# Denominators a pair later in an attention kernel: both late key sums on VectorE, the shift spread on ScalarE, and another order at the seams

## The reference, cut to what matters

```python
x = x + 0.5 * ffn(layernorm(x))
x = x + attn(layernorm(x))
x = x + 0.5 * ffn(layernorm(x))

# attn: 16 heads of 64
q = q * cos + rotate_half(q) * sin + fenc
k = k * cos + rotate_half(k) * sin + fenc
dots = einsum('bhid,bhjd->bhij', q, k) * 64 ** -0.5
attn = softmax(dots, axis=-1)
out = einsum('bhij,bhjd->bhid', attn, v)
return out.reshape(b, n, 1024) @ w_out.T + b_out
```

## Time and profile before

| what | value |
|---|---|
| median of 3 runs (lowest, highest) | 1273.29 us (1272.16, 1274.07) |
| the profiled execution's own time | 1275.4 us |
| its span in the profile | 1273.6 us |
| PE busy | 1229.2 us, 97% |
| DVE busy | 955.6 us, 75% |
| POOL busy | 896.2 us, 70% |
| ACT busy | 627.9 us, 49% |
| chain that ended last | PE 86%, issue 4%, POOL 4%, DVE 3% |

### The profile page before, as it was taken

One profiled execution on the slowest core, in us unless ns is written; L12 is line 12 of the kernel. 1 busy time (PEld: TensorE's weight loads), 2 busy tenths in 40 slices (PEclk: granted clock), 3 DMA queues, 4 the chain that ended last, 5 costly groups with the idle time before them and its releaser, 6 DMA issues.

```text
span 1273.6 us, 20947 instructions
## 1 busy us (share of the span) xinstructions
PE 1229.2 (97%) x7346; PEld 780.9 (61%) x7346; DVE 955.6 (75%) x1443; ACT 627.9 (49%) x917; POOL 896.2 (70%) x652
## 2 busy tenths in 40 slices
PE   4999999899999999999999999999999987999998
PEld 3666666556666566666666666666666644666665
DVE  6656777778888888888888888888787865656632
ACT  3444522455555546455556555555555552443422
POOL 0443346788998898898898899889889932543353
PEclk9999999999999999999999999999999998999999
DMA  5353150132333333232323232323232310443150
GB/s 169 134 183 91 43 150 17 33 66 54 70 58 67 61 64 64 63 65 59 69 60 68 60 68 60 68 57 70 51 77 52 76 19 19 141 142 108 43 158 17
DMA packets 118677, 95.35 MB, mean 75 GB/s; under 512 B 75760, under 2 KB 85008, under 8 KB 118320
## 3 DMA queue, kind: packets, MB, share of 16 engines
q1 hardware_dynamic: 118064, 93.75, 30.2%
q10 hardware_dynamic: 512, 0.26, 0.1%
HBM read 57.53 MB, written 2.88 MB: 47 GB/s over the span
## 4 chain that ended last, share of the span: by engine, by line
PE 86%; issue 4%; POOL 4%; DVE 3%; DMA 1%; ACT 1%; SPq 0%; POOLq 0%; DVEq 0%; ACTq 0%
PE banks L1156 16%; PE banks L453 15%; PE banks L1135 13%; PE banks L466 10%; PE banks L1074 6%; PE banks L994 5%; PE banks L1172 5%; PE banks L1140 4%; PE banks L1181 4%; PE banks L1002 3%; POOL work L1428 2%; PE banks L1113 1%; POOL turn L1418 1%; PE banks L415 1%; PE banks L408 1%
## 5 line engine op out<-in xcount | busy, mean ns | idle before, releaser
L1006 DVE TENSOR_REDUCE neg_max<-banks 128x2 f32<-128x1024 f32 x256 | 305.1, 1226 | 11.0 <-PE banks L994 6.2
L1256 ACT ACTIVATE work<-banks 128x1024 f32<-128x1024 f32 x256 | 262.4, 1026 | 93.8 <-PE banks L1140 77.6
L1156 PE MATMUL banks<-work 128*64 128x512 f32 x1024 | 233.8, 598 | 2.0 <-ACT work L1256 1.1
L1428 POOL TENSOR_TENSOR work<-work 128x1024 f32<-128x1024 f32 x64 | 159.6, 2494 | 81.4 <-PE banks L1156 81.3
L1418 POOL TENSOR_TENSOR turn<-turn,side_turned 128x512 f32<-128x512 f32 x128 | 163.7, 1301 | 29.8 <-DMA side_turned<-side 29.6
L1412 POOL TENSOR_TENSOR turn<-turn,fenc 128x512 f32<-128x512 f32 x128 | 162.8, 1291 | 2.0 <-DVE side L1327 2.0
L1423 POOL TENSOR_TENSOR qk_l<-turn,qk_h 128x512 fp32r<-128x512 f32 x128 | 161.8, 1285 | 2.8 <-ACT qk_h L983 2.8
L1156 PEld LDWEIGHTS banks<-work 128*64 128x64 f32 x1024 | 68.0, 136 | 135.0 <-issue 109.9
L1348 DVE TENSOR_TENSOR work<-work 128x1024 f32<-128x1024 f32 x64 | 105.4, 1647 | 38.2 <-PE banks L1156 38.2
L807 POOL TENSOR_TENSOR o_raw<-o_raw,work 128x512 f32<-128x512 f32 x52 | 66.9, 1289 | 89.8 <-DVE o_raw L723 89.7
L807 POOL TENSOR_TENSOR work<-work 128x512 f32<-128x512 f32 x44 | 56.5, 1292 | 96.7 <-DVE work L723 51.7
(11 more groups left out here) (177 smaller groups left out, 2459.3 us busy)
## 6 DMA issues: line engine op xcount, KB each, us to landing
work<-share SPq DMA_DIRECT2D x32, 1024.0 KB, 9.4
side_turned<-side SPq DMA_DIRECT2D x256, 128.0 KB, 3.1
rec_all<-rec_d SPq DMA_DIRECT2D x128, 128.0 KB, 3.0
x_tok<-in_x SPq DMA_DIRECT2D x8, 256.0 KB, 6.5
out<-x_tok SPq DMA_DIRECT2D x8, 256.0 KB, 9.4
work<-in_w_gate_up SPq DMA_DIRECT2D x1, 1280.0 KB, 7.2
work<-in_w_qk SPq DMA_DIRECT2D x1, 1024.0 KB, 9.7
den_d<-den_rows ACTq DMA_DIRECT2D x64, 4.0 KB
```

What stands on the lines that cost most here:

```text
L1006: return nc.vector.tensor_reduce(neg_max[:, g % 2, qt::DH], of, AX.X, ALU.max, negate=True)
L1156: ins = nc.tensor.matmul(o_bank(g)[OWN[h], :], v_all[:, kt, n * DH:(n + 1) * DH], pt[:, g % 2, kt, h * T:(h + 1) * T], start=(kt == 0), st ...
L1256: nc.scalar.activation(pt[:, g % 2, kt, :], S[kt].rearrange("p h q -> p (h q)"), ACT.Exp, scale=QSCALE).then_inc(s["probs"], 1)
L1428: nc.gpsimd.tensor_tensor(pt[:, g % 2, 2, :], pt[:, g % 2, 2, :], pt[:, g % 2, 3, :], ALU.add).then_inc(s["second_sum"], 1)
```

## The change

It has these parts, of which the first four are in the attention stage.

- The denominators of pair `g` are formed a period later (in period `g+2`), from one tile instead of two, for all pairs but the last two (`lazy`). VectorE adds tile 3 to tile 2 (`late_sum`, after V has been applied to these two, which now come first in `ORDER`), GpSimd adds tile 1 to tile 0 into tile 3 (`early_sum`), and in the next period VectorE adds tile 3 to tile 2 again (`total`). TensorE multiplies tile 2 alone with ones.
- Everything behind the denominators moves a period later too: copying, DMAs, reciprocals, normalising, output projection, residual. `o_raw` has three places for that.
- `spread_maxima` moves from VectorE to ScalarE, as four activations of 128 columns.
- In period 61 the odd tokens of `ffn2`, and at the program's start those of `ffn1`, move from VectorE (`first_tokens`) to ScalarE (`odd_tokens`).
- The order at the seams: positions and shares of the routing one unit later, routing steps spread over other units, the early layer norm one unit sooner, and another order in attention's tail.

```diff
-LOGITS_AT, EXPS_AT, POSITIONS_AT, SHARES_AT = 8, 10, 14, 16
+LOGITS_AT, EXPS_AT, POSITIONS_AT, SHARES_AT = 8, 10, 15, 17
-FIRST_ROUTE_AT = {0: range(4, 12), 1: range(12, 19), 2: range(19, 22), 3: range(22, 24)}
+FIRST_ROUTE_AT = {0: range(4, 12), 1: range(12, 19), 2: range(19, 22), 4: range(22, 24)}
-        o_raw = sb("o_raw", [P, 2, T])
+        o_raw = sb("o_raw", [P, 3, T])
-            first_positions, first_shares = (1, 2) if last else (3, 4)
+            first_positions, first_shares = (2, 3) if last else (4, 5)
...
+                def odd_tokens():
+                    act.wait_ge(s["normed"], 1)
+                    for t in range(TT):
+                        n = TT + t
+                        ins = nc.scalar.activation(xn2[1][:, t, :], x_tok[:, 1, t, :], ACT.Identity,
+                                                   scale=rs_c[:, n:n + 1], bias=shift_c[:, n:n + 1])
+                    ins.then_inc(s["xn_first"], 1)
...
-            EARLY_NORM_AT = {-14: range(0, 4), -13: range(4, 7), -12: range(7, 10), -11: range(10, 13), -10: range(13, 16)}
+            EARLY_NORM_AT = {-15: range(0, 4), -14: range(4, 7), -13: range(7, 10), -12: range(10, 13), -11: range(13, 16)}
...
+            ORDER = (2, 3, 0, 1)
+
+            def lazy(g):
+                return g < N - 2
...
                 def denominators(g, p):
                     pe.wait_ge(s["v_ready"], min(p + 4, B * 2 * TT))
                     at_least(pe, s["den_copied"], g)
-                    pe.wait_ge(s["first_sum"], g + 1)
-                    pe.wait_ge(s["second_sum"], g + 1)
-                    for n, kt in enumerate((0, 2)):
+                    if lazy(g):
+                        pe.wait_ge(s["total"], g + 1)
+                    else:
+                        pe.wait_ge(s["late_sum"], g + 1)
+                        pe.wait_ge(s["early_sum"], g + 1)
+                    tiles = (2,) if lazy(g) else (2, 3)
+                    for kt in tiles:
...
-                    if exists(p - 3):
-                        project_out(p - 3, p)
-                    if exists(last):
-                        denominators(last, p)
+                    if exists(p - 4):
+                        project_out(p - 4, p)
...
+                    if exists(p - 2):
+                        denominators(p - 2, p)
...
+                def spread_maxima(g):
+                    act.wait_ge(s["shift_ps"], g + 1)
+                    at_least(act, s["scores"], (g - 1) * TT)
+                    for t in range(TT):
+                        ins = nc.scalar.activation(shift[:, g % 2, t * P:(t + 1) * P], MT, ACT.Copy, scale=own_rows[:, t:t + 1])
+                    ins.then_inc(s["shift_ready"], 1)
...
-                def first_sum(g):
-                    dve.wait_ge(s["first_applied"], g + 1)
-                    nc.vector.tensor_tensor(pt[:, g % 2, 0, :], pt[:, g % 2, 0, :], pt[:, g % 2, 1, :],
-                                            ALU.add).then_inc(s["first_sum"], 1)
+                def add_tiles(g):
+                    return nc.vector.tensor_tensor(pt[:, g % 2, 2, :], pt[:, g % 2, 2, :], pt[:, g % 2, 3, :], ALU.add)
+
+                def late_sum(g):
+                    dve.wait_ge(s["last_applied"], g + 1)
+                    add_tiles(g).then_inc(s["late_sum"], 1)
+
+                def total(g):
+                    dve.wait_ge(s["early_sum"], g + 1)
+                    dve.wait_ge(s["late_sum"], g + 1)
+                    add_tiles(g).then_inc(s["total"], 1)
...
-                    if exists(p - 2):
-                        reciprocals(p - 2)
+                    if exists(p - 3):
+                        reciprocals(p - 3)
+                    if exists(p - 2):
+                        total(p - 2)
                     end_norm(p)
...
                     if exists(p - 1):
-                        first_sum(p - 1)
-                    if exists(nxt):
-                        spread_maxima(nxt)
+                        late_sum(p - 1)
...
-                def second_sum(g):
+                def early_sum(g):
                     pool.wait_ge(s["o_ps"], g + 1)
-                    nc.gpsimd.tensor_tensor(pt[:, g % 2, 2, :], pt[:, g % 2, 2, :], pt[:, g % 2, 3, :],
-                                            ALU.add).then_inc(s["second_sum"], 1)
+                    pool.wait_ge(s["late_sum"], g + 1)
+                    nc.gpsimd.tensor_tensor(pt[:, g % 2, 3, :], pt[:, g % 2, 0, :], pt[:, g % 2, 1, :],
+                                            ALU.add).then_inc(s["early_sum"], 1)
```

136 lines of the change are left out of this document (73 added, 63 removed).

## The result

The changed kernel takes 1326.04 us (median of 4 runs, 1322.95 to 1327.34), the kernel before 1272.80 in the runs beside it: a ratio of 1.0412, 95% interval 1.0393 to 1.0431. The forecast was 1296 with a range of 1275 to 1318. Sign and mechanism came out as argued; the time lies outside the range.

What follows compares the result with a forecast made beforehand. TensorE bounds the kernel before, GpSimd second; after the change, GpSimd and VectorE's sums in turn. 1275.4 + 25.6 + 7 - 9.9 = 1298.1 us, less 2.1 for the median: 1296 us, range 1275 to 1318.

Steps and rivals of the forecast that it cites:

- (1): TensorE in attention: half the denominator matmuls go in 62 lazy pairs, saving 0.45 us a period, hidden behind GpSimd.
- (2): Attention: VectorE's second key sum also blocks GpSimd for 1.00 us, making the period 13.27 us, +25.6 us in all.
- No order of the instructions gets below this sum: Attention: GpSimd and VectorE are served in turn, so reordering cannot bring the period below 13.27 us.
- the front term: Seven batch-turning periods: spreading on ScalarE delays rope, residual and TensorE by 1.0 us each, +7 us, bounds 0 and 11.
- The upper bound of the term: Attention: each VectorE sum costs GpSimd its full 1.22 us, giving +51 us instead of +25.6.
- Before: 11.27 + 1.00 = 12.27: Kernel before, attention: GpSimd's work plus one blocking sum stays under the 12.83 us period, hidden in 1.39 us of waits.
- the second sum finds 0.39 us of them: Attention: GpSimd's gaps already hide the first VectorE sum, leaving 0.39 us for the second; argued against a faster result.
- case C: Rival, about as now: full seam gains, cheaper sums or VectorE's total landing in GpSimd's waits; 1262 to 1272 us, chance 0.06.
- (3): Attention: spreading on ScalarE takes 1.4 us and delays the seven batch-turning periods, +7 us.
- (5): Seams at the program's start and attention's ends: reordering removes TensorE waits, -9.9 us in sum.
- (4): Attention: third raw-output buffer, reciprocals and normalising a period later remove VectorE's waits for DMA; counted as nothing.
- case A: The forecast itself: GpSimd and VectorE's sums in turn set the period at 13.0 to 13.4 us; 1281 to 1304, chance 0.72.

Runs made afterwards that it cites:

- e3: The changed kernel with VectorE's `total` replaced by a one-operand reduction over as many columns, part of the denominators left out: 1271.66 us, ratio 0.9973.
- e6: The kernel before with one more VectorE addition of two SBUF operands, 1024 columns, per period, result unused: 1309.93 us, ratio 1.0272.
- e7: The kernel before with one more VectorE reduction of one SBUF operand, 1024 columns, per period, result unused: 1275.76 us, ratio 1.0010.
- e15: The changed kernel with GpSimd's Fourier additions cut to half the positions, the rest left out: 1282.99 us, ratio 1.0073.
- e5: The changed kernel with a buffer of its own for GpSimd's sum, which no longer waits for the late sum: 1323.32 us, ratio 1.0392.
- e14: The changed kernel with VectorE's late sum put ahead of the total: 1315.44 us, ratio 1.0326.
- e4: The changed kernel with the spreading of the maxima back on VectorE: 1317.78 us, ratio 1.0349.
- e11: The kernel before with part of the change's seams, the last `first_sum` between routing steps, positions and shares later in `ffn2`: 1269.24 us, ratio 0.9965.
- e12: The kernel before with one more VectorE addition of two SBUF operands, only 512 columns, per period, result unused: 1286.31 us, ratio 1.0109.

## Why the forecast had the sign and not the size

By its own terms, against the profiled executions. The forecast's sum for the changed kernel, 1298.1 us, stands against 1324.93: 26.8 us short.

- **(1) Half the denominators' matmuls.** Forecast 0.45 us a period, hidden. Found: it comes to light only when GpSimd is relieved (e3's median period 12.35).
- **(2) Two meetings set the period, 13.27 us, +25.6.** The mechanism is shown from both sides: e6 and e7 by adding it, e3 by taking it away, e15 by the load. Its price is right too, if both forms of it are counted: in the change GpSimd is blocked for 1.20 us a period and waits 0.83 for the late sum, 2.03 for the 2.00 taken. What failed is the step "No order of the instructions gets below this sum", read as if the kernel could also reach it: the sum 11.27 + 2.00 has no other wait of GpSimd, while the forecast's own sign allowed up to 25 us of them. Found were 19.4 us in the stretch, 0.33 a period: 12.6 for the turned side, 4.9 for TensorE, 1.9 for rope. The table below has this split for five kernels. With the 7 of the front term, which is one of these waits, 12.4 us were missing, and 1.8 more for the 2.03: 14.2 us of the shortfall. The upper bound of the term (1.22 us a sum, +51) would have covered the stretch, though for another reason.
- **A price misread in the kernel before.** "Before: 11.27 + 1.00 = 12.27" is not what its rows say: GpSimd was busy for 663.22 us, 11.43 a period. The first sum had hardly used the slack of 1.39, so "the second sum finds 0.39 us of them" is wrong as well. The error does not touch the 13.27, but it hid that the cost of a meeting depends on who is loaded.
- **The new wait.** The forecast did not name the wait of GpSimd's sum for the late sum in its sum (case C touches it). It is GpSimd's longest (48.3 us). By itself it is not the cause, as e5 shows; its order relative to the total is worth 0.16 us a period (e14).
- **(3) Spreading on ScalarE.** Its four instructions of 372 ns each overlap and take 1.13 us (1.4 taken). The +7 us for the seven periods that turn a batch was nearly right, and by the path that was forecast as far as rope: by e4, 5.6 us. On TensorE they do not stand out (13.79 us in the mean, the others 13.62), since the delay reaches it a period later through GpSimd and not through the residual.
- **(5) The seams, -9.9.** Found: -1.8 ahead of the stretch and +4.5 behind it, +2.7, so 12.6 us of the shortfall. Single executions scatter here: the ten kernels with lazy pairs have 268.36 to 270.65 us ahead of the stretch, 269.7 in the mean, the four with the old order 270.7, so the gain is nearer 1.0 than 1.8. One term was misread from the start: at the program's start the odd tokens do not move to ScalarE (only in period 61), against what the change's description says further up, and the +1.5 for it never was; TensorE's first projection waits 1.5 us for `x_lo` as before. The mask's wait falls from 2.1 to 1.3. At the far end "each wait may have another behind it" was the right doubt with too small a price: the four waits of 8.4 us went, and 9.7 and 3.6 came. Without the lazy pairs this end does give what was forecast (e11, -7.0 behind the stretch for the -6).
- **(4)** was costed at nothing, "waits of an engine off the bound", and the DMAs were said to "cover themselves". That holds in the steady stretch; it fails in the tail, where the order on SyncE and the place of pair 61's reciprocals on VectorE make the 9.7 us.
- In case A "1304 with the larger front cost" doesn't come out of its terms: 11 us instead of 7 gives 1300.

A period of GpSimd, in us; "blocked" is its busy time less 11.27 (the work, taken as the same in all), "other waits" is what is left, all rounded:

| run | own work | blocked | waiting for the late sum | other waits | period |
|---|---|---|---|---|---|
| the forecast | 11.27 | 2.00 | 0 | 0 | 13.27 |
| the change | 11.27 | 1.20 | 0.83 | 0.33 | 13.64 |
| e14_late_first | 11.27 | 1.40 | 0.43 | 0.37 | 13.47 |
| e4_spread_dve | 11.27 | 1.33 | 0.78 | 0.15 | 13.53 |
| e5_early_own | 11.27 | 1.79 | 0 | 0.55 | 13.61 |
| e6_before_sum | 11.27 | 1.86 | 0 | 0.38 | 13.51 |

The Trainium skill (SBUF — State Buffer, "SBUF: two separate sides") has the lock for the whole instruction. By that the steady period would be an estimated 13.71 against 13.64 measured, which looks like agreement. It isn't one: the blocking in e6 is 0.93 us a sum and not 1.22, and the rest of the period is idle time.

**Left open**: why the other waits are 0.55 us a period in e5 and 0.15 in e4; the runs give their names, not what makes rope late outside the seven periods. And whether a tail exists in which the lazy pairs hide their DMA chain: two tries did not find one. Taking the reciprocals of pair 62 just when their denominators land, or dropping the laziness some pairs earlier, was not tried.

## What to carry to other kernels

Count the elementwise work of VectorE with two SBUF operands and that of GpSimd as one queue: here each sum of 1024 columns on VectorE cost a loaded GpSimd 0.9 to 1.0 us, blocked or waiting, while a reduction over as many columns cost nothing. A trade of TensorE time (0.45 us a period) for such a sum loses once GpSimd's slack (1.39 us here) is used up, and somewhat before (e12). The loss is larger than the plain sum of work and blocking, since in none of the five kernels of the table the loaded engine ran without a gap: add the waits that remain, 0.15 to 0.55 us a period here. And postponing a chain through DRAM by a period is free only where another period follows; at the end of a stage look for what is queued behind the instruction that receives it, and for what the DMA queue itself waits for before it fetches.

## What the runs showed of the hardware

- A two-operand addition on VectorE blocks GpSimd, a reduction of one operand in SBUF does not: turned parts 1790 against 1281 ns in e6 and e7, where only that instruction differs.
- Where both engines have work ready, they alternate, one instruction each: neither is shut out, and each pays for about one instruction of the other (4.24 us for two sums, 4.51 for two turned parts, at 658; VectorE's start at 658.57 and 660.52, GpSimd's at 659.45 and 661.69).
- Small steps pay for the meeting as well. A VectorE step on 8 columns takes 0.16 us where it is not held (L278 at 648.28), and 1.24 and 1.27 in the rows from the timeline at 645, beside the two turned parts. One of these two (L277) has a single operand, so the count of operands is not the whole rule.
- Instructions of VectorE with one operand in PSUM and one in SBUF are not held: rope took 1.21 to 1.22 us and the residual 0.68 in both kernels, while GpSimd was busy for 89 and 91% of the time (at 658, rope's two instructions of 1.23 and 1.21 us run beside GpSimd's sum of 2.36).
